# Feature-interaction tower on one core: the first chunk in two halves, weights on ScalarE's queue, idle passes on TensorE

## The reference

```python
x0 = x = stack(tbl_f[ids[:, f]])                 # (512, 64, 16)
h1 = einsum('bid,bjd,ijn->bnd', x0, x,  W0)      # W0 (64*64, 128)  "layer 0"
h2 = einsum('bid,bjd,ijn->bnd', x0, h1, W1)      # W1 (64*128, 128)
h3 = einsum('bid,bjd,ijn->bnd', x0, h2, W2)
z  = concat([sum_d h1, sum_d h2, sum_d h3])      # (512, 384)
h  = relu(concat([z, dense_ctx]) @ W_top1 + b_top1)
h  = relu(h @ W_top2 + b_top2);  y = h @ W_top3  # (512, 1)
```

## Time and profile before

| | |
|---|---|
| median of 3 runs | 1179.36 us |
| the profiled execution | 1178.92 us, its span 1177.1 us |
| TensorE (PE) busy | 1114.9 us, 95% of the span |
| VectorE (DVE) / GpSimd (POOL) / ScalarE (ACT) busy | 877.9 / 761.5 / 561.0 us |
| mean granted TensorE clock | 0.993 |
| first bank filled from | 61.23 us |

### The profile page before, as it was taken

The page is one execution under the profiler, slowest core; times in us unless marked ns, Lnnn a source line. Parts: engine busy times, 40 slices in busy tenths (PEclk is TensorE's granted clock), DMA queues, the critical chain, the costliest instruction groups (busy, mean ns, idle before and its releaser), DMA issues.

```text
span 1177.1 us, 20381 instructions
## 1 busy us (share of the span) xinstructions
PE 1114.9 (95%) x4628; PEld 786.1 (67%) x4628; DVE 877.9 (75%) x2746; ACT 561.0 (48%) x1812; POOL 761.5 (65%) x660
## 2 busy tenths in 40 slices
PE   0679999999999999999999999999999999999999
PEld 0256666666677766766767766666667777666765
DVE  3468878888886588878886578878787687878840
ACT  2134555454553445546454354555554355545631
POOL 6547686858585485768766387676868358545640
PEclk9989999999999999999999999999999999999989
DMA  7873414243443424343333534224243532423000
GB/s 223 178 177 73 97 36 110 52 99 72 91 116 73 111 63 90 80 90 77 66 87 85 139 77 92 61 48 105 47 106 98 146 72 36 117 77 118 2 1 0
DMA packets 125018, 102.62 MB, mean 87 GB/s; under 512 B 76929, under 2 KB 81857, under 8 KB 124258
## 3 DMA queue, kind: packets, MB, share of 16 engines
q1 hardware_dynamic: 116706, 99.17, 34.5%
q0 software_dynamic: 8192, 2.11, 2.0%
HBM read 97.04 MB, written 4.20 MB: 86 GB/s over the span
## 4 chain that ended last, share of the span: by engine, by line
PE 87%; DVE 5%; POOL 3%; issue 3%; DMA 2%; DVEq 0%; ACT 0%; SPq 0%; POOLq 0%
PE tps L630 20%; PE tps L632 19%; PE tps L631 19%; PE acc L602 18%; PE side L657 5%; DVE parts_sb L451 3%; POOL rows_sb L346 3%; PE side L644 2%; PE acc L598 1%; PE side L652 1%; PE tps L712 1%; DMA rows_sb<-tables,rows_now_sb 1%; DVE z_sb L430 1%; PE side L611 0%; DVE parts_sb L447 0%
## 5 line engine op out<-in xcount | busy, mean ns | idle before, releaser
L451 DVE SCALAR_TENSOR_TENSOR parts_sb<-tps,xcol_sb,parts_sb 128x128 f32<-128x128 f32 x2432 | 670.5, 343 | 191.2 <-PE tps L632 187.8
L518 ACT ACTIVATE y_sb<-tps,xcol_sb 128x128 f32<-128x128 f32 x1536 | 438.2, 369 | 524.0 <-PE tps L632 523.7
L630 PE MATMUL tps<-w_hi_sb,h_hi_sb 128*128 128x512 f32 x1024 | 509.9, 498 | 17.8 <-DVE parts_sb L451 15.1
L632 PE MATMUL tps<-w_hi_sb,h_lo_sb 128*128 128x512 f32 x1024 | 405.9, 396 | 0.0
L631 PE MATMUL tps<-w_lo_sb,h_hi_sb 128*128 128x512 f32 x1024 | 404.9, 395 | 0.0
L346 POOL DMA_INDIRECT rows_sb<-tables,rows_now_sb x256 | 246.1, 962 | 77.4 <-issue 49.1
L630 PEld LDWEIGHTS tps<-w_hi_sb,h_hi_sb 128*128 128x128 f32 x1024 | 193.7, 189 | 135.5 <-DVE parts_sb L451 52.3
L602 PE MATMUL acc<-prod_sb,w_sb 128*128 128x512 f32 x512 | 266.1, 605 | 5.9 <-DVE prod_sb L424 5.9
L361 POOL TENSOR_TENSOR ysum_sb<-y_sb 128x1024 f32<-128x1024 f32 x64 | 153.4, 2397 | 177.8 <-ACT y_sb L518 177.1
L631 PEld LDWEIGHTS tps<-w_lo_sb,h_hi_sb 128*128 128x128 f32 x1024 | 193.9, 189 | 87.7 <-issue 57.4
L632 PEld LDWEIGHTS tps<-w_hi_sb,h_lo_sb 128*128 128x128 f32 x1024 | 193.5, 189 | 45.3
(11 more groups left out here) (47 smaller groups left out, 361.8 us busy)
## 6 DMA issues: line engine op xcount, KB each, us to landing
roll_sb<-x_scratch SPq DMA_DIRECT2D x256, 256.0 KB
w_sb<-w_rows SPq DMA_DIRECT2D x40, 256.0 KB, 3.5
rows_sb<-tables,rows_now_sb POOLq DMA_INDIRECT x256, 4.3
gsum_sb<-w_rows SPq DMA_DIRECT2D x8, 512.0 KB, 4.6
xx_sb<-x_scratch SPq DMA_DIRECT2D x16, 256.0 KB, 2.7
x_scratch<-rows_sb SPq DMA_DIRECT2D x30, 128.0 KB, 3.8
roll_sb<-x_scratch SPq DMA_DIRECT2D x32, 64.0 KB
w_sb<-w_tiles SPq DMA_DIRECT2D x1, 1024.0 KB, 5.4
```

The source lines that it names most:

```text
L451: dve.scalar_tensor_tensor(part, bank, scale, part, ALU.mult, ALU.add).then_inc(d_done, 1)
L518: done = act.activation(y[:, pair % Y_RING, half * CH + u * NF:half * CH + (u + 1) * NF], tps[:, p % RING, u * NF:(u + 1) * NF], ACT.Copy, ...
L630: pe.matmul(bank, h1_hi[:, par, cols], w1_hi[:, of], start=True, stop=False, skip_group_check=True)
L632: pe.matmul(bank, h1_lo[:, par, cols], w1_hi[:, of], start=False, stop=True, skip_group_check=True).then_inc(t_ready, 1)
```

## The change

Chunk 0 is cut into two halves of 256 columns (16 samples). Each half is gathered by 8 indirect DMAs of its own order of ids (`first_ids`, 16 samples x 8 fields each) and stored into a DRAM scratch of its own (`x_halves`, rows of 1 KB); its rolls, products, float32 tiles, rounding and sums run on 256 columns. Half 0 goes through layer 0 ahead of place 0; half 1 inside chunk 0, at the places `LATE_...`, and places 0 to 31 use half 0's h1, 32 to 63 half 1's. The pieces of chunks 1 and 2 in chunk 0 move to later places (`FIRST_...`). The weights and constants are issued by ScalarE on its own hardware queue, all at once; TensorE does 20 passes into the bank ring whose results nobody reads, once the first part of W1 is rounded. GpSimd gathers chunk 1 without waiting for chunk 0 to land. The cut diff (the halves' semaphores, the column arguments of `product`, `split_h1`, `copy_xx`, `round_h1`, `copy_xcol`, and the waits by half in `take_bank`, `scale_bank`, `fill_bank` are left out):

```diff
+WARM = 20
+LATE_XX_AT, LATE_XCOL_AT = 4, 6
+LATE_PROD_AT = tuple(range(6, 6 + 2 * GROUPS, 2))
+LATE_L0_AT = tuple(p + 2 for p in LATE_PROD_AT)
+LATE_H1_AT = 27
+FIRST_L0_AT = tuple(range(32, 32 + 3 * GROUPS, 3))
+FIRST_ROLL_AT = (30, 33, 36, 39, 42)
+FIRST_GATHER_AT = tuple(range(16, 16 + 2 * STEPS, 2))
+FIRST_STORE_AT, FIRST_XX_LOAD_AT = 48, 50
+FIRST_NEXT_ROLL_AT = (51, 52, 53, 54)
 # SyncE, prologue
+            sp.dma_start(first_ids[:], ins["first_ids"]).then_inc(first_ids_loaded, 16)
+            sp.dma_start(first_table_rows[:], ins["first_table_rows"]).then_inc(first_ids_loaded, 16)
             sp.dma_start(ids[:], ins["ids_steps"]).then_inc(ids_loaded, 16)
             sp.dma_start(table_rows[:], ins["table_rows"]).then_inc(ids_loaded, 16)
-            (W0, constants, and four times: two parts of W1, wait, store a quarter)
+            sp.wait_ge(first_gathered[0], 16 * HALF_STEPS)
+            store_half(0)
+            sp.wait_ge(first_stored[0], 32)
+            sp.dma_start(xx[:, HALVES[0]], x_halves[0]).then_inc(first_xx_loaded, 16)
             for g in range(GROUPS):
                 if g >= ROLL:
+                    sp.wait_ge(first_prod_ready, g - ROLL + 1)
+                load_roll(x_halves[0], g, (g - GROUPS) % ROLL, first_roll_loaded, HALVES[0])
+                if g == ROLL - 1:
+                    sp.wait_ge(first_gathered[1], 16 * HALF_STEPS)
+                    store_half(1)
+            sp.wait_ge(first_stored[1], 32)
+            sp.dma_start(xx[:, HALVES[1]], x_halves[1]).then_inc(xx_loaded, 16)
+            for g in range(GROUPS):
+                if g < ROLL:
+                    sp.wait_ge(first_prod_ready, GROUPS + g - ROLL + 1)
+                else:
                     sp.wait_ge(prod_ready, g - ROLL + 1)
+                load_roll(x_halves[1], g, g % ROLL, roll_loaded, HALVES[1])
             sp.wait_ge(gathered[1], 16 * STEPS)
             store_rows(1, 1, slice(0, STEPS), x_stored)
 # GpSimd, prologue (first_rows = first_ids + first_table_rows)
+            for half in range(2):
+                for s in range(half * HALF_STEPS, (half + 1) * HALF_STEPS):
+                    pool.indirect_dma_start(... first_rows[:, s:s + 1] ...).then_inc(first_gathered[half], 16)
             pool.wait_ge(ids_loaded, 32)
-            for k in range(QUARTERS):
-                gather(0, 0, quarter(k), first_gathered[k])
-            for k in range(QUARTERS):
-                pool.wait_ge(first_gathered[k], 16 * STEPS // QUARTERS)
             gather(1, 1, slice(0, STEPS), gathered[1])
 # VectorE, prologue: parts 0 to 3 of W1's rest, then
             for g in range(GROUPS):
+                first_product(g)
+                if g % 2 == 1:
+                    w1_rest(W1_PARTS // 2 + g // 2)
+            first_split_h1()
 # ScalarE, prologue
+            (dma_start of w0, w0_back, w0_end, 3 constants, 8 parts of W1)
+            (round W1 parts 0 to 3; copy half 0's xx and xcol; parts 4 to 7; round half 0's h1)
 # TensorE, prologue
+            pe.wait_ge(w1_hi_ready, 1)
+            for k in range(WARM):
+                pe.matmul(tps[:, k % RING, :], w1_hi[:, 0:P], w1_hi[:, 0:CH], start=True, stop=True)
+            pe.wait_ge(first_xx_loaded, 16)
+            turn_blocks(range(SUB // 2), first_xcol_filled)
             pe.wait_ge(w0_loaded, 48)
             pe.wait_ge(w0_summed, 1)
             for g in range(GROUPS):
-                layer0(-2, 0, g, (0, 1))
+                first_layer0(g)
 # chunk 0, each engine: half 1's pieces at LATE_..., chunk 1's and 2's at FIRST_...
```

More of the change, by code:

```diff
@@ L68, with l0_at, product_at, l0_second @@
 NEXT_ROLL_AT = (47, 49, 51, 53)
-def quarter(k):
-    return slice(k * STEPS // QUARTERS, (k + 1) * STEPS // QUARTERS)
+HALF = CH // 2
+HALVES = (slice(0, HALF), slice(HALF, CH))
+HALF_F = P // (SAMPLES // 2)
+HALF_STEPS = FIELDS // HALF_F
+WARM = 20
[8 more added lines that the diff above has]
+FIRST_NEXT_ROLL_AT = (51, 52, 53, 54)
+def l0_at(q):
+    return FIRST_L0_AT if q < 0 else L0_AT
+def product_at(q):
+    return tuple(p - 4 for p in FIRST_L0_AT) if q < 0 else PROD_AT
+def l0_second(q):
+    return 1 if q < 0 else L0_SECOND
 def is_a(p):
@@ L240, in store_rows, with store_half, load_roll @@
                                  rows[:, slot, steps, :]).then_inc(stored, 16)
-            def load_roll(t, g, slot):
+            def store_half(half):
+                for copy in range(2):
+                    dst = x_halves[half, copy * FIELDS:(copy + 1) * FIELDS, :]
+                    sp.dma_start(dst.rearrange("(s f) (b d) -> (f b) s d", f=HALF_F, d=DIM),
+                                 rows[:, 0, half * HALF_STEPS:(half + 1) * HALF_STEPS, :]).then_inc(first_stored[half], 16)
+            def load_roll(x, g, slot, loaded, cols=slice(0, CH)):
+                width = cols.stop - cols.start
@@ L302, in chunk @@
                         store_rows(t + 2, odd, slice(0, STEPS), x_stored)
-                    if p == XX_LOAD_AT and gathers(t):
+                    if p == xx_load_at and gathers(t):
                         sp.wait_ge(x_stored, t * 32 + 64)
@@ L391, in chunk @@
                             finish_block(q - 1, t - 1, SUB - 1)
[L392 to L393 removed]
+                    if p in gather_at and gathers(t):
+                        step = gather_at.index(p)
                         if step == 0:
@@ L455, in _, with w1_rest @@
             dve.tensor_tensor(w0[FIELDS:P, 0, :], w0[FIELDS:P, 0, :], w0_back[FIELDS:P, 0, :], ALU.add).then_inc(w0_summed, 1)
-            for k in range(W1_PARTS):
+            def w1_rest(k):
                 dve.wait_ge(w1_hi_ready, k + 1)
@@ L609, in turn_x, with turn_blocks @@
                 pe.sem_inc(pe_passed, 1)
-                for s in range(SUB):
+                turn_blocks(range(SUB // 2 if isinstance(t, int) and t == 0 else 0, SUB), xcol_filled)
+            def turn_blocks(blocks, filled):
+                for s in blocks:
                     mm = pe.transpose(side[:, 1, s * FIELDS:(s + 1) * FIELDS], xx[0:FIELDS, s * P:(s + 1) * P],
                                       ident[0:FIELDS, 0:FIELDS])
-                mm.then_inc(xcol_filled, 1)
+                mm.then_inc(filled, 1)
             def fill_bank(q, t, p):
@@ L701, in chunk @@
                         contract_w2(bt, F_AT.index(p))
-                    if p in L0_AT and not last:
-                        layer0(q, t + 1, L0_AT.index(p), (0,))
-                    if p - L0_SECOND in L0_AT[:WHOLE] and not last:
-                        layer0(q, t + 1, L0_AT.index(p - L0_SECOND), (1,))
+                    if p in at and not last:
+                        layer0(q, t + 1, at.index(p), (0,))
+                    if p - second in at[:WHOLE] and not last:
+                        layer0(q, t + 1, at.index(p - second), (1,))
                     fill_bank(q, t, p)
```

218 lines of the change are left out of this document (159 added, 59 removed).

## The result

The changed kernel takes 1166.69 us (median of 4 runs, 1164.01 to 1167.73), the kernel before 1179.08 beside it: ratio 0.9891, 95% interval [0.9878, 0.9904]. The forecast was 1166.6. The profiled execution of after (the changed kernel) took 1167.73 us (span 1165.9), that of before 1178.92 (span 1177.1).

The account below looks back on a forecast made before the run. TensorE sets the pace from the first bank; ahead stands a chain of gathers, stores, xx, rolls, products. First bank 44.4 + 76.1 put place 4 of chunk 1 at 120.5, 12.35 earlier: 1178.92 - 12.35 = 1166.6 us, range 1158 to 1174.

Parts of the forecast that it names:

- (a): GpSimd's first gather: small id loads share DMA engines with ScalarE's weights, 1.5 us later (ends -0.3 and 3.2).
- (b): Half 0's eight gathers: denser weights add 0.5 us (0 to 1.4), so its store starts at 21.6.
- C: Rival: DMA engines serve ScalarE's weights ahead of GpSimd's gathers; half 0's store 3 to 18.5 us worse; chance 0.05.
- (c): Half 0's store writes 2048 packets in 3.3 us; its xx is issued at 24.9.
- (d): From xx's issue to the first product: half the bytes save 1.8 of 5.87 us, first product at 29.0.
- (e): Half 0's roll pairs every 1.27 us (ends 0.95 and 2.54); product 4 at 36.7 behind half 1's gathers.
- A: Rival: a packet costs the same at 1 KB as at 2 KB; only 2.3 us earlier, 1176.6; chance 0.12.
- (f): Last product's end to first bank: 1.6 us instead of 4.08; first bank at 44.4, 16.8 earlier.
- First bank to place 4: Stretch up to place 4 of chunk 1: 71.62 - 5.46 - 2.35 + 7.3 + 1.5 + 3.5 = 76.1 us.
- B: Rival: x of chunk 2 comes 6 us later than worked out, each costing TensorE one; 1172.6; chance 0.12.
- D: Rival: the split fails, TensorE starts places 0 to 31 early and stands at place 8 for half 1; 1179; chance 0.03.
- Behind it nothing is changed: Behind place 4 of chunk 1 nothing changes, so the change is worth what it moves that row: 12.35 us.

Follow-up runs that it names:

- run 7: Changed kernel with ScalarE's weights held until the first ids have landed: 1165.42 us, 0.9878.
- run 6: Kernel before with only the weights and constants moved to ScalarE's queue, chunk 0 whole: 1181.39 us, 1.002.
- run 12: Changed kernel with the edits of run 7, run 8 and run 11, and two of the three new tiles allocated last: 1158.58 us, 0.9826.
- run 8: Changed kernel with half 1's store behind all of half 0's rolls instead of behind the fourth: 1165.31 us, 0.9888.
- run 9: Changed kernel without TensorE's 20 idle passes: 1167.46 us, 0.9896.
- run 10: Changed kernel with 52 idle passes instead of 20, to last until x comes: 1169.53 us, 0.9919.
- run 2: Changed kernel with its three new tiles allocated last, so that the other tiles lie where they lay before: 1165.71 us, 0.9879.
- run 3: Kernel before with one unused tile of 192 bytes a partition behind `rows_now`: 1180.51 us, 1.0015.
- run 1: The changed kernel again, unchanged: 1167.66 us, 0.9898.
- run 5: Kernel before with one unused tile of 64 bytes a partition: 1172.18 us, 0.994.
- run 4: Kernel before with chunk 0's row numbers in their own tile and chunk 1's gathers not waiting for chunk 0's landing: 1170.70 us, 0.9936.
- run 11: Changed kernel with ScalarE's copy of chunk 2's x at place 60 of chunk 0 instead of 56: 1165.42 us, 0.9881.

## Why the prediction was right, and where only its sum was

The mechanism and the main size were right: first bank at 44.02 (44.4 predicted), half pairs, no stall at place 8, the gap near place 60. That 1166.6 met 1166.69 is in part luck: place 4 of chunk 1 was 2.5 us better than worked out, 3.6 us were lost behind it, where the prediction said that nothing is changed, and the profiled execution lies 1.0 us above the median.

- **(a) First gather: mis-sized.** +1.5 was taken, +2.9 measured (7.19 against 4.29), near the upper end of 3.2. Run 7 takes it away; run 6 shows such a delay without the halves. The Trainium skill, page "DMA: Bandwidth & Descriptors", section "Queues, rings and completion order", states that a DMA engine takes turns between its queues, a packet of several descriptors at a time. By that rule the prediction had estimated 3.2; the trace, with 2.9, agrees with the estimate.
- **(b) Half 0's store: 20.14, 21.6 predicted.** The late first gather was made good: half 0 is stored 2.24 behind the start of its eighth gather (17.90), not 4.45 and more. In the DMA view the weights move at some 410 GB/s, not at the 326 of the earlier trace rows, and are over by 18.8; only half of half 0's 256 gather packets have moved by 18 us, the other half follow by 20.1. So the weights do hold the gathers back, though not wholly, as C feared; C's price (a store at 24.7 or later) was not paid because they were over sooner. In runs 7 and 12 the eighth gather starts 3.5 us earlier, at 14.4, among weights that last to 20.7 and 21.3, and the store goes no earlier (20.34 and 20.76).
- **(c), (d): close.** The store was seen after 3.02 us and the first product started 3.87 behind `xx`'s issue; 3.3 and 4.1 were predicted.
- **(e) Pairs: the value was right, its lower end not.** SP issues the first four pairs without a gap, 5.24 us for 8 issues, 1.31 per pair; so its issuing sets the pace here, and 0.95 could not be reached. A, with pairs at 2.54 and nothing saved in (d), is out. Product 4 was predicted at 36.7 and came at 35.59; the wait behind half 1's gathers was in the sum, and run 8 shows that it need not be there: 3.1 us.
- **(f) The tail: 1.8**, 1.6 predicted (41.81 + 0.41 to 44.02).
- **The idle passes: nothing**, as predicted, and for its reason (runs 9, 10).
- **First bank to place 4: 74.01, 76.1 predicted.** VectorE's +1.5 (its own terms, 30.5 against 29.4, make it 1.1) did not come: TensorE's only two gaps are 0.38 and 1.19. The x of chunk 2 was late as described, but the last gather was stored 2.4 after its issue, not 3.4, and the store seen after 4.5, not 5.1: 1.2 instead of 3.5. B, which had this x 6 us late, is out. TensorE's busy time rose by 6.6 (65.88, by the window of before from 61.23 to 132.85, to 72.44), where 7.3 less the 2.35 of the low clock made 4.95; of these 1.6 the shift and half 1's turn of x explain some 0.5, the rest is open. D is out: no gap stands at place 8.
- **"Behind it nothing is changed": wrong.** The three new tiles shift the tiles behind them, and the chunk takes longer (runs 2, 3): 1.87 us over fourteen chunks, although before had a low-clock stretch of 3.4 us there and after none. The rest of the 3.6 is mostly the longer low-clock stretch of the tail, 10.2 us instead of 6.8, which belongs to the execution (run 1).
- **The yardstick itself**: place 4 at 132.85 was late for that order of instructions (run 5); if that belongs to the execution, 14.8 us overstates the gain by up to 2.5.

## What to carry to other kernels

Before a new tile goes into the middle of an allocation, put it last, or time the kernel with an unused tile in its place: here an unused 64 bytes was worth more than any single wait that was removed. A small load on which the first work hangs can be held up by bulk traffic on another queue; whether letting it go first pays depends on the next wait (2.3 us in run 7, nothing in run 12). A wait on an in-order queue belongs behind everything that doesn't need it. When two fixes shorten the same wait, only one of them counts.

## What the runs showed of the hardware

The placement of tiles in SBUF changes the length of a chunk on TensorE. Below are the distance from one mark to the next and, for every kernel with that shift, the fourteen chunks from the mark of chunk 1 to that of chunk 15, with the instructions of before and of after mixed:

| shift of the tiles behind `rows_now` | chunk, us | fourteen chunks, us |
|---|---|---|
| 0 bytes | 64.58 (before), 64.52 (run 2) | 951.2 to 951.7 (before, runs 2, 6) |
| 64 bytes | 64.26 (run 4), 64.23 (run 5), 64.28 (run 12) | 947.1 to 948.0 (runs 4, 5, 12) |
| 192 bytes | 64.71 (after), 64.71 (run 1), 64.70 (run 3) | 953.1 to 954.8 (after, runs 1, 3, 7 to 11) |

The three groups do not overlap. The difference lies in the fp32r passes themselves: over some 150 steps between neighbouring passes behind the mark of chunk 1, one pass starts on average 232 ns behind the other at 0 bytes (before, run 2), 230 at 64 (runs 5, 12) and 233.4 at 192 (after, run 3). Why a shift does this no run shows.
